# Self-attention stage: scores issued one step ahead, score rows as tokens, V in both partition halves with zero blocks

## The reference, cut to what matters

```python
qkv = x @ W_w.T + W_b                       # 256 -> 768; 16 heads of 16
attn = einsum('bhqd,bhkd->bhqk', q, k) / sqrt(256)
attn = where(causal, -inf, attn) + bias     # bias: [head, query, key], the same for all batches
w = softmax(attn, axis=-1)
o = einsum('bhqk,bhkd->bqhd', w, v)         # back to [token, 256]
y = x + o @ proj_w.T + proj_b
out = (y - mean) / sqrt(var + eps) * ln_g + ln_b
```

## Time and profile before

| what | value |
|---|---|
| median of 3 runs | 1731.11 us (1729.69 to 2875.7) |
| profiled execution | 1730.49 us, span 1728.7 us, mean granted clock 0.925 |
| busy over the span | PE 84%, PEld 59%, DVE 63%, ACT 52%, POOL 49% |

### The profile page before, as it was taken

How to read it: one execution, slowest core, us unless ns; L and a number is a source line. 1 busy time by engine, 2 the same in 40 slices (tenths; PEclk the granted TensorE clock), 3 DMA queues, 4 the chain that set the end, 5 groups by cost and what they waited for, 6 DMA issues and landing times. The chain is left out here.

```text
span 1728.7 us, 55875 instructions
## 1 busy us (share of the span) xinstructions
PE 1450.7 (84%) x24601; PEld 1018.8 (59%) x24601; DVE 1081.6 (63%) x1736; ACT 900.0 (52%) x1196; POOL 839.4 (49%) x555
## 2 busy tenths in 40 slices
PE   3789999999999999999999999999655655457607
PEld 2357777677776777766777767777424444333206
DVE  7656666666666666666666666666353444586985
ACT  1446555566556665566665556656433322143752
POOL 5567655666655666556665566653053443202000
PEclk9899999999999999999999999999876876678958
DMA  5544544334444344443454534543122110010001
GB/s 171 134 118 103 126 115 136 105 98 123 120 112 133 98 117 123 114 134 98 108 129 108 143 99 101 128 115 69 31 70 52 26 38 1 1 37 0 1 0 49
DMA packets 90688, 154.94 MB, mean 90 GB/s; under 512 B 17280, under 2 KB 55816, under 8 KB 90448
## 3 DMA queue, kind: packets, MB, share of 16 engines
q1 hardware_dynamic: 89088, 150.40, 33.4%
q10 hardware_dynamic: 1360, 0.98, 0.2%
HBM read 60.95 MB, written 2.20 MB: 37 GB/s over the span
## 5 line engine op out<-in xcount | busy, mean ns | idle before, releaser
L639 DVE TENSOR_REDUCE MXP<-W_PS 128x1 f32<-128x512 f32 x768 | 499.2, 688 | 283.4 <-PE W_PS L451 283.4
L535 ACT ACTIVATE PR<-S_PS 128x1024 f32<-128x1024 f32 (+1 forms) x416 | 424.9, 1023 | 258.6 <-PE S_PS L399 250.8
L345 POOL TENSOR_TENSOR K_HI<-K,MCOL 128x512 f16<-128x512 f32 (+1 forms) x224 | 219.0, 978 | 425.3 <-ACT K L543 424.0
L347 POOL TENSOR_TENSOR K_LO<-K,K_HI 128x512 f16<-128x512 f32 (+1 forms) x224 | 291.8, 1302 | 17.6
L451 PE MATMUL W_PS<-STK,QS 105*128 105x512 f16 (+1 forms) x1024 | 269.8, 335 | 9.0 <-POOL STK L372 4.8
L399 PE MATMUL S_PS<-QS,STK 105*128 105x128 f16 (+1 forms) x3328 | 256.0, 220 | 1.0 <-DVE QS L653 1.0
L414 PEld LDWEIGHTS O_PS<-PR,V 128*17 128x17 f32 x13312 | 191.0, 98 | 79.2 <-issue 59.1
L414 PE MATMUL O_PS<-PR,V 128*17 128x64 f32 x13312 | 231.3, 220 | 7.6 <-ACT PR L535 7.5
L434 PE MATMUL W_PS<-WV_HI,CTX_HI 128*128 128x256 f16 (+1 forms) x832 | 228.3, 274 | 1.6 <-DVE WV_LO L612 1.4
L434 PE MATMUL W_PS<-WV_HI,CTX_LO 128*128 128x256 f16 (+1 forms) x832 | 227.7, 274 | 0.0
L434 PE MATMUL W_PS<-WV_LO,CTX_HI 128*128 128x256 f16 (+1 forms) x832 | 227.6, 274 | 0.0
(11 more groups left out here) (243 smaller groups left out, 1713.3 us busy)
## 6 DMA issues: line engine op xcount, KB each, us to landing
CTX<-in_ctx_t SPq DMA_DIRECT2D x64, 800.5 KB, 5.9
STK<-K_HI SPq DMA_DIRECT2D x256, 128.0 KB, 2.6
STK<-K_HI SPq DMA_DIRECT2D x256, 72.1 KB, 2.1
STK<-K_LO SPq DMA_DIRECT2D x128, 128.0 KB, 2.6
STK<-K_LO SPq DMA_DIRECT2D x128, 72.1 KB, 2.1
QSTK<-STK SPq DMA_DIRECT2D x12, 192.0 KB
SQS<-QK_HI SPq DMA_DIRECT2D x32, 64.0 KB, 2.0
KZ<-QK_HI SPq DMA_DIRECT2D x64, 32.0 KB, 2.0
```

The lines of the kernel that those rows point to most:

```text
L345: pool.tensor_tensor(K_HI[:, m, lo:hi], k32, zero, ALU.add).then_inc(k_hi, 1)
L347: pool.tensor_tensor(K_LO[:, m, lo:hi], k32, K_HI[:, m, lo:hi], ALU.subtract).then_inc(k_lo, 1)
L535: nc.scalar.activation(PR[0:m, par, :], S_PS[par][0:m, :], ACT.Exp).then_inc(p_sb, 1)
L639: dve.tensor_reduce(MXP[:, j, at:at + 1], bank[:, :], AX.X, ALU.max).then_inc(mx_done, 1)
```

## The change

Score rows become tokens (batch, query) and columns (pair, head, key), so one matmul with 128 moving columns serves both heads and the bias tile grows to 128 x 1024. V for each batch is computed into both partition halves: V[:, group parity, batch, pair, 32], where rows 0 to 63 hold the even head in columns 0 to 15 and rows 64 to 127 the odd head in columns 16 to 31, the other blocks zero. One matmul then gives 32 output rows (both heads), so outputs fill 2 instead of 4 column groups and the projection contracts over 2 instead of 4 blocks. VS, its copies and the constant row are gone; the V bias is folded through the projection into a row BP, which POOL adds to XN. PE issues scores of s+1 at the head of step s. DVE sums s-1 right after the maximum of s. ACT does BESIDE evictions ahead of the exponential. SP sends high parts first. Zeros come by ACT (KZ group 0) and by DMA (V, KZ group 1). The gate weight's load and work move into steps 3 to 9.

```diff
+BESIDE = {0: TN2, 1: QK2 (0,1), 2: QK2 (2,3), 3: TN3, 4: QK3 (0,1), 5: QK3 (2,3),
+    6: [("VV", 2, 0)], 7: [("VV", 2, 1)], 8: WT 0,1, 9: WT 2,3, 10: [("VV", 3, 0)], 11: [("VV", 3, 1)], ...}
+RESIDUAL = {0: 0, 1: 1, 4: 2, 7: 3}
 ...
 # SP
+        sp.wait_ge(sm["zero"], 1)
+        zero(V[:, 0] ..., 2, zeroed[0])
         for r in range(TILES // 4):
+            if r == 1:
+                zero(KZ[:, 1] ..., 4, zeroed[1])
+                zero(V[:, 1] ..., 2, zeroed[1])
-            sp.wait_ge(sm["qk_lo"], 4 * r + 2)
+            sp.wait_ge(sm["qk_hi"], 4 * r + 2)
             if r >= 2:
                 sp.wait_ge(sm["s_ps"], 4 * (r - 1))
+            queries(0, QK_HI); queries(1, QK_HI)
+            sp.wait_ge(sm["qk_hi"], 4 * r + 4)
+            if r == 0:
+                sp.wait_ge(sm["zero"], 5)
+            elif r == 1:
+                sp.wait_ge(zeroed[1], 32)
+            keys(0, QK_HI); keys(2, QK_HI)
+            sp.wait_ge(sm["qk_lo"], 4 * r + 4)
+            queries(2, QK_LO); keys(1, QK_LO)
+            if r == 1:  # load of w_gate into WRAW
+                sp.dma_start(WN..., dram["w_gate"]...).then_inc(sm["in_wg"], 16)
 # PE, VV unit: 48 matmuls of 128 columns for 12 of 256
+                for b in range(4):
+                    for e, (h, w, k) in enumerate(...6...):
+                        for a in range(2):
+                            last = pe.matmul(bank[SQ * a:SQ * (a + 1), b * P:(b + 1) * P], XR[:, r, h, k, cols], w[...a...], ...)
+        def scores(t):
+            need(pe, sm["t_a"], t)
+            for j in range(PAIRS):
+                for w in range(2):
+                    last = pe.matmul(S_PS[SQ * w:SQ * (w + 1), j * P:(j + 1) * P], SQS[0:96, r % 2, j, cols],
+                                     KZ[0:96, r % 2, j, :, cols], start=True, stop=True, skip_group_check=True)
+        scores(0)
         for s in range(STEPS):
-            if live(s): ... scores of s
+            if live(s + 1):
+                scores(s + 1)
             if live(s - 2):
-                    for h in range(H): ... O_PS[row:row + DH] from VS, PT      (32 matmuls)
+                    for w in range(2): ... O_PS[row:row + 32] from V, PT       (16 matmuls)
-                for g in range(4): projection
+                project(OT[:, t % 2])                                          (2 matmuls)
 # ACT, step s
             PT, OT copies of s-2 (OT 256 columns for 512)
-            VS copies of s-1
+            BESIDE evictions of s (not XT)
             exponential of s
 # POOL: memsets gone; in steps: xp adds of 128x1024 at s in RESIDUAL, gate multiplies at s == 5 and s == 6
 # DVE, VV eviction: 2 tensor_scalar of 64 x 512 for 1 of 128 x 512, the first of a group waits for zeroed / pv
 # DVE, step s
             add, maximum of s
+            sum, reciprocal of s-1
             residual add, statistics of s-3; BESIDE
+            if s == 3:
+                dve.wait_ge(sm["in_wg"], 16)
+                (reduce, scale, reciprocal of the gate weight)
+            if s == 6:
+                dve.wait_ge(sm["wg_int"], 1)
+                (round, clip)
             scale_rows, add_rows as before
-            sum, reciprocal of s-1
```

More of the change, by code:

```diff
@@ L885, in self_attention @@
     stacked = [sem(nc, ctx, f"stacked{r}") for r in range(TILES // 4)]
-    N_SMALL = 5
+    zeroed = [sem(nc, ctx, f"zeroed_{s}") for s in ("first", "second")]
     PARTS = 36
+    N_SMALL = 7
     units = SETUP + [x for s in range(STEPS) for x in BESIDE.get(s, [])] + ENDING
@@ L931, in _, with zero @@
-        sp.dma_start(WN.rearrange("p (f d) -> p f d", f=FT), dram["w_gate"].rearrange("(f p) d -> p f d", p=P)).then_inc(sm["in_wg"], 16)
-        sp.dma_start(WP[:, :, :], dram["wp"]).then_inc(sm["in_wp"], 16)
+        sp.dma_start(WP[:, :, :], dram["wp"].rearrange("(g p) n -> p g n", p=P)).then_inc(sm["in_wp"], 16)
+        sp.wait_ge(sm["zero"], 1)
+        def zero(dst, n, done):
+            rows = dst.shape[0]
+            sp.dma_start(dst.rearrange("p (n z) -> p n z", n=n), ZERO[0:rows].unsqueeze(1).broadcast_to([rows, n, PAIRS * 2 * SQ]))\
+                .then_inc(done, 16)
@@ L933, in _ @@
+        zero(V[:, 0].rearrange("p t j c -> p (t j c)"), 2, zeroed[0])
         for r in range(TILES // 4):
             u = r % 2
-            sp.wait_ge(sm["qk_lo"], 4 * r + 2)
[L936 to L939, removed]
-                    sp.dma_start(SQS[32 * q:32 * q + 32, u, c::4, :], part[32 * c:32 * c + 32, u, 0:2, :]).then_inc(stacked[r], 16)
-            sp.wait_ge(sm["qk_lo"], 4 * r + 4)
@@ L942, in _, with queries @@
[L942 to L945, removed]
+            if r == 1:
+                zero(KZ[:, 1].rearrange("p j a c -> p (j a c)").bitcast(F32), 4, zeroed[1])
+                zero(V[:, 1].rearrange("p t j c -> p (t j c)"), 2, zeroed[1])
+            def queries(q, part):
+                for c in range(4):
+                    sp.dma_start(SQS[32 * q:32 * q + 32, u, c::4, :], part[32 * c:32 * c + 32, u, 0:2, :]).then_inc(stacked[r], 16)
@@ L946, in _, with keys @@
+            def keys(q, part):
+                for c in range(4):
                     for a in range(2):
@@ L998, in setup @@
                 last.then_inc(sm["xt_ps"], 1)
+        def scores(t):
+            r, lo = t // 4, t % 4 * P
+            if t % 4 == 0:
+                pe.wait_ge(stacked[r], 16 * PARTS)
+            need(pe, sm["t_a"], t)
+            for j in range(PAIRS):
+                for w in range(2):
+                    cols = slice(lo + w * SQ, lo + (w + 1) * SQ)
+                    last = pe.matmul(S_PS[SQ * w:SQ * (w + 1), j * P:(j + 1) * P], SQS[0:96, r % 2, j, cols],
+                                     KZ[0:96, r % 2, j, :, cols], start=True, stop=True, skip_group_check=True)
+            last.then_inc(sm["s_ps"], 1)
@@ L1000, in _, with project @@
+        def project(outs):
+            for g in range(KT):
+                last = pe.matmul(Y_PS[:, 0:D], outs[:, g, :], WP[:, g, :], start=(g == 0), stop=(g == KT - 1))
+            return last
         for x in SETUP:
             setup(x)
+        pe.wait_ge(sm["in_wp"], 16)
+        pe.wait_ge(sm["bp_row"], 1)
+        project(OT[:, 0]).then_inc(sm["bp_ps"], 1)
+        scores(0)
         for s in range(STEPS):
[L1003 to L1007, removed]
+            if live(s + 1):
+                scores(s + 1)
+            if live(s - 2):
+                t = s - 2
+                pe.wait_ge(sm["pt"], t + 1)
+                pe.wait_ge(sm["v_sb"], 2 * (t // 2 + 1))
+                need(pe, sm["ot"], t)
@@ L1015, in _ @@
[L1015 to L1028, removed]
+                        row, col = 32 * (j % 4), j // 4 * P + w * SQ
@@ L1029, in _ @@
+                        last = pe.matmul(O_PS[row:row + 32, col:col + SQ], V[:, t // 4 % 2, 2 * (t % 4) + w, j, :],
+                                         PT[:, t % 2, j, w * SQ:(w + 1) * SQ], start=True, stop=True, skip_group_check=True)
                 last.then_inc(sm["pv"], 1)
@@ L1032, in _ @@
                 if t == 0:
-                    pe.wait_ge(sm["in_wp"], 16)
+                    pe.wait_ge(sm["bp_row"], 2)
                 pe.wait_ge(sm["ot"], t + 1)
                 need(pe, sm["y_sb"], t)
-                for g in range(4):
-                    last = pe.matmul(Y_PS[:, 0:D], OT[:, t % 2, g, :], WP[:, g, :], start=(g == 0), stop=(g == 3))
-                last.then_inc(sm["y_ps"], 1)
+                project(OT[:, t % 2]).then_inc(sm["y_ps"], 1)
             for x in BESIDE.get(s, []):
@@ L1098, in normal_again @@
                     .then_inc(sm["xn3"], 1)
+        nc.scalar.activation(ZERO, CST[:, C_HM:C_HM + 1].broadcast_to([P, PAIRS * 2 * SQ]), ACT.Copy, scale=0.0).then_inc(sm["zero"], 1)
         act.wait_ge(sm["ln2"], LN_ROOT)
         nc.scalar.activation(SD[:, :], VE[:, :], ACT.Sqrt).then_inc(sm["root2"], 1)
+        for i in range(3):
+            zero_keys(i)
         for x in SETUP:
             setup(x)
-        act.wait_ge(sm["init"], 3)
+        nc.scalar.activation(VU[:, 0:1], CST[:, C_HM:C_HM + 1], ACT.Exp)
         for s in range(STEPS):
@@ L1114, in _ @@
                 need(act, sm["y_ps"], t - 1)
[L1115 to L1122, removed]
+                if t == 0:
+                    act.wait_ge(sm["bp_ps"], 1)
+                nc.scalar.activation(OT[:, t % 2, :, :], O_PS[:, 0:D].rearrange("p (g r) -> p g r", g=KT), ACT.Copy).then_inc(sm["ot"], 1)
+            for x in BESIDE.get(s, []):
+                if x[0] != "XT":
+                    setup(x)
             if live(s):
@@ L1220, in _ @@
         normal(range(0, 4))
-        normal(range(4, 8))
         setup(SETUP[0])
```

209 lines of the change are left out of this document (114 added, 95 removed), and 8 rows, old and new, of tables (BESIDE, SETUP).

## The result

| | before | changed |
|---|---|---|
| median | 1732.12 us (4 runs, 1729.69 to 2875.7) | 1664.84 us (4 runs, 1663.34 to 1666.51) |
| profiled execution | 1730.49 us, span 1728.7 | 1663.34 us, span 1661.2, granted clock 0.932 |

The ratio is 0.9616, with a 95% interval of 0.9597 to 0.9635: 67 us less, for 65 forecast (1667). It leaves out the one slow run of 2875.7. The parts did not all come as forecast, and most of the gain has another source than the halved matmuls.

The account below looks back on a forecast made before the run. A chain across engines bounds the steps, with no engine full, and SP's copies bound what precedes them. 1730.5 less 68 by the stage's earlier end, plus 4 for the lock, gives 1666.5 profiled, median 1667; range 1645 to 1703.

Parts of the forecast that it names:

- Setup, 9.9: Setup: SP starts its 36 copies at 1263.4, not 1273.30, so first scores come at 1289.2, a gain of 9.9 us.
- the same cover: Setup: SP's queue of copies up to 1289.2, taken to hide the added PE and DVE work.
- Tile 4: Group 1's first tile: scores at 1325.0 behind the copies, bias add at 1332.3 behind the gate weight's load and work.
- Zero copies, 16: Group 1's stack: two zero copies ahead of the keys take 16 us, ends 14.5 and 27, counted one for one.
- The steps, 150.9 or 130.4: Tile 4's bias add to the stage's end: 150.9 us with PE at 1.2 GHz, 130.4 at 2.4 GHz.
- the table: Steps from tile 4 on: five stretches timed at both PE clocks, each with what paces it; sums 150.9 and 130.4.
- 68: Stage's end, 1540.9 before: gain in us, taken as the middle of 57.7 and 78.2 for the two PE clocks.
- Rival 3: Steps: the turn is only shortened, not opened; each keeps its chain; gain 32 us, 1699; chance 0.13.
- Rival 5: Steps: P V and projection not halved, 1.9 us a step back on PE in about six steps; 1678; no separate chance.
- The lock, 4: Row work of steps 13 to 15: DVE held by POOL's passes, 4 us in all, from 0 to 11.4.
- Sum: Whole kernel: 1730.5 - 68 + 4 = 1666.5 us for the profiled execution, median of the runs 1667.

Follow-up runs that it names:

- zero_early: Changed kernel with all three zero copies issued together at the start of setup, instead of group 1's two behind group 0's stack; 1653.29 us.
- zero_gate_early: Changed kernel with all zero copies at the start of setup and the gate weight's load also issued ahead of group 0's stack; 1653.31 us.
- before_reordered: Kernel before with only the two orders changed: scores one step ahead, DVE's row sum right behind the maximum; layouts, projection, setup as before; 1660.47 us.

## Why the prediction was right, and where it was not

**Setup, 9.9.** Right for the scores: forecast at 1289.2, measured 1289.17 with 11.11 us waiting for KZ. The gain did not reach the first bias add, which came 4.6 us later than before.

**The step that failed** is "DVE's bias scaling doubles and evictions of V become two; hidden by the same cover." I had costed the zero copies on SP's queue alone, for the keys, and not asked who else waits for them. DVE does, in setup's last units, and the first bias add is queued behind it. The price is 11.5 us (zero_early); in the range it stood at nothing.

**Tile 4 came right by another cause.** Forecast: scores at 1325.0, held by the stack; the add at 1332.3, behind w_gate. Measured: 1325.99 and 1333.70. But SP issued the last key copy by 1318.69 (the row of KZ<-QK_LO starts at 1313.65 and lasts 5.04), the scores waited for no DMA, and the wait for w_gate costs nothing (zero_gate_early). The 44.5 us from the first scores to this add are DVE's wait and then four steps in a row. What I wrote, "Tiles 1 to 3 are done by about 1306", was wrong: tile 0's add had only begun. Two errors cancelled.

**Zero copies, 16.** SP starts the keys at 1300.94, 13.2 us after the first was issued and 12.5 after the second, below my lower end of 14.5. The 8 query issues did not run freely beside them: they took 11.68 us (row at 1289.12), where the 8 of group 0 took 5.17. The Trainium skill, SBUF — State Buffer, Summary, gives 436 GB/s, by which 2560 KB would take 6 us as an estimate, 8 with the 2.0 of a small copy; the trace does not agree: 2560 KB in 13.2 us is 200 GB/s.

**The steps, 150.9 or 130.4.** From tile 4's add to the stage's end 139.5 us were measured (1333.70 to 1473.20), the middle that I took being 140.7. By stretches, 28.0 (33.9 or 25.3), 8.9 (9.0 or 6.4), 27.3 (31.7 or 25.8), 30.3 (29.4 or 27.4) and 45.1 (46.9 or 45.5). The grants of 0.81, 0.82, 0.68 and 0.65 lie between the levels, as the table supposed. The middle is in part luck, since PE's terms were too low. The 1.99 of the earlier trace rows for a full projection is its length at the higher level (before_reordered at grant 1.00); at the lower it takes 3.78 (its row at 1436.24). So a step of the changed kernel costs PE 1.06 + 1.10 + 2.08 + 1.91 = 6.2 at the lower level, for 4.9 in the table, and 0.64 + 0.69 + 1.13 + 1.09 = 3.6 at the higher, for 2.9. P V fell from 1.91 to 1.10 and from 1.09 to 0.69, not by half. (DVE's four distances add up to 4.81, not 4.85.) So the stage's end at 1473.2 is where 68 puts it (1540.9 - 68 = 1472.9).

**What pays it** I had partly wrong. The table charges PE with P V and projection halved alike, 0.93 and 1.0 a step. The runs give the projection 15 us and P V none. And with halved work the grant is lower (0.82 for 1.00 from tile 7 to 12), so that, beside the V units and the gate work that the steps now carry, nothing is left of it against before_reordered: from tile 4's add to tile 12's that kernel takes 57.1 us (1335.55 to 1392.68), the changed one 64.1. The changed kernel gives back 7.0 there and 8.7 more between first scores and tile 4's add (44.5 against 35.8), and wins 10.6 at the first scores (1299.77 against 1289.17) and 4.8 from tile 12 on, so that the stages end 0.3 us apart. The traces show this split; how much of the 7.0 is V units, gate work or clock was not tried and stays open.

**Rival 3** (1699, the turn only shortened) fell, for the reason given against it: "it waits for its place in DVE's order alone." Undoing the place of the row sum alone gives back 54 us of the 67. ACT's evictions ahead of the exponential do make the sum wait in four places, 10.0 us in all, and the gain stands in spite of it. **Rival 5** put both halves at 11 us in six steps, 1678; doubling both gave 1680.25. The number is near by luck: P V's half gives nothing and the projection's works in all 16 steps.

**The lock, 4.** DVE's first line of the row work (L1318, two SBUF inputs) has one instruction of 2.05 us among 16, two of 0.59 and 0.57 (1423.83 and 1441.45), the others 0.47 to 0.48; its mean is 0.584, where before it was 0.471:

```profile
L1318 DVE SCALAR_TENSOR_TENSOR XN<-XN,MV,LG x16: 468/468/2051, 1413.7 to 1466.7; 128x256 f32<-128x256 f32 x16
```

That is 16 x 0.113 = 1.8 us, 2 less than forecast. The long one starts at 1432.59, just behind the start of POOL's pass of 1432.46 + 1.90, and ends 0.28 us behind its end; so do the other two, which start late in their POOL passes. By the Trainium skill, SBUF — State Buffer, Who interferes with whom, the later one blocks for all of the other: the three rows agree. But this line met a POOL pass only three times, and but once at its start.

**Sum.** 1663.34 for the profiled execution against 1666.5.

## What to carry to other kernels

When a chain across engines sets the pace, look first at where each link stands in its engine's list: one row sum, ready long before but queued behind an add that waits for another engine, held 54 us of this kernel. Taken alone in the kernel before, that move and scores one step ahead gave as much as the whole change. For each new wait, list every engine that waits for the same event, not only the queue that you are costing. And try the reordering alone before rebuilding layouts around it.

## What was not expected of the hardware

- Less work on PE did not always mean less time on PE: from tile 7 to 12 the full matmuls ran at grant 1.00 (PE busy 24.2 of 31.8 us), the halved ones at 0.82 (26.9 of 36.1, other units among them), and a whole second P V pass in 16 steps cost 0.35 us between medians (1679.90 and 1680.25).
- A matmul that repeats the one just before it into the same place is slow: P V with each of 16 matmuls doubled at once 2.41 us, the same 32 in two passes 1.17.
- SP issues copies at 0.64 to 0.68 us each, large or small (0.61 and 0.66 for 1536 and 1024 KB), and ACT's queue issues beside it at the same pace. But behind the two large copies the small ones stalled: 8 in 11.68 us, the longest 2.78.
